# Decoder layer on one core: the feed-forward's W2 sums move to the retention's PSUM bank, W is split in another order, and TensorE transposes the identity in its waits

## What is computed

```python
x = layernorm(x + retention(x))        # 16 heads, decay mask, group norm per head, silu gate, wo
x = layernorm(x + mamba(ctx, z=x))     # conv 4, softplus step, 16 states, scan over 256 tokens
x = layernorm(x + moe_lora(x))         # W1, W3, W2 (F = 896), top 2 of 8 experts of rank 32

# retention
scores = einsum('bhnd,bhmd->bhnm', q, k) * dmask
ret = einsum('bhnm,bhmv->bhnv', scores, v)
norm = (ret - mean) * rsqrt(var + EPS) * gn_w + gn_b
out = silu(x @ wg + bg) * norm @ wo + bo
# mamba, per token
state = state * exp(d_t * A) + (d_t * u_t) * B_t;  y_t = sum(state * C_t)
y = (y + D * u) * silu(z)
# feed-forward, for each of the two experts e of a token, with its weight rw
x1 = x @ W1.T + lora1_e(x);  x3 = x @ W3.T + lora3_e(x);  x2 = silu(x1) * x3
out += (x2 @ W2.T + lora2_e(x2)) * rw
```

## Time and profile before

| | us |
|---|---|
| timed runs, median of 3 (lowest, highest) | 475.28 (475.27, 477.44) |
| the profiled execution, whole | 477.86 |
| the profiled execution, span from first to last instruction | 476.1 |
| mean granted TensorE clock in it | 0.934 |

### The profile page before, as it was taken

One profiled execution on the slowest core, in us unless ns is written; L12 is line 12 of the kernel. 1 busy time (PEld: TensorE's weight loads), 2 busy tenths in 40 slices (PEclk: granted clock), 3 DMA queues, 4 the chain that ended last, 5 costly groups with the idle time before them and its releaser, 6 DMA issues.

```text
span 476.1 us, 6961 instructions
## 1 busy us (share of the span) xinstructions
PE 410.4 (86%) x2488; PEld 336.6 (71%) x2488; DVE 340.3 (71%) x630; ACT 209.8 (44%) x497; POOL 231.6 (49%) x214
## 2 busy tenths in 40 slices
PE   3879674499899979997999979998999798799993
PEld 2645554367678968875779877876789687699992
DVE  3445975835889997768989996778889985632224
ACT  2699672547453332458534323476623322221010
POOL 5054766403936775116764954047566851041221
PEclk9989757759899999999999989999999989979999
DMA  6958040030013220030112220020121200000000
GB/s 227 140 223 326 2 154 22 0 92 23 1 46 88 76 69 23 1 92 23 45 66 70 66 61 19 17 86 12 67 89 44 67 1 1 0 23 1 1 1 23
DMA packets 14531, 28.46 MB, mean 60 GB/s; under 512 B 1816, under 2 KB 5152, under 8 KB 14240
## 3 DMA queue, kind: packets, MB, share of 16 engines
q1 hardware_dynamic: 13440, 23.26, 16.9%
q10 hardware_dynamic: 1056, 4.75, 2.7%
HBM read 26.56 MB, written 1.44 MB: 59 GB/s over the span
## 4 chain that ended last, share of the span: by engine, by line
PE 48%; DVE 26%; issue 13%; ACT 7%; POOL 3%; DMA 1%; SPq 1%; POOLq 0%; DVEq 0%; ACTq 0%
PE gen L880 14%; PE xf L880 14%; DVE ring L1427 10%; PE acc L880 8%; PE a2p L880 8%; PE ret L880 3%; DVE fth L1658 2%; DVE ring L1437 2%; ACT decay L597 2%; DVE ring L1486 1%; DVE cv L1369 1%; DMA wattn_sb<-in_wattn 1%; DVE work L1669 1%; POOL ring L497 1%; POOL wsplit L460 1%
## 5 line engine op out<-in xcount | busy, mean ns | idle before, releaser
L880 PE MATMUL xf<-am,wsplit 128*128 128x256 f32 x672 | 99.5, 300 | 0.0
L880 PEld LDWEIGHTS xf<-am,wsplit 128*128 128x128 f32 x672 | 89.2, 199 | 4.9 <-issue 4.3
L453 POOL TENSOR_TENSOR ring<-cv,brow 128x512 f32<-128x512 f32 x48 | 75.7, 1594 | 20.0 <-PE acc L880 19.7
L597 ACT ACTIVATE decay<-dt_w,nega 128x255 f32<-128x255 f32 x128 | 57.7, 500 | 58.1 <-DVE ring L1427 51.5
L1427 DVE TENSOR_TENSOR_SCAN ring<-decay,ring 128x512 f32<-128x512 f32 x48 | 76.5, 1593 | 0.0
L566 POOL TENSOR_TENSOR work<-work,ratioT 128x256 f32<-128x256 f32 x28 | 29.9, 1067 | 74.5 <-DVE work L1669 62.8
L880 PE MATMUL a2p<-work,wff_sb 128*128 128x256 f32 x224 | 60.4, 394 | 3.1 <-POOL work L566 3.1
L845 ACT ACTIVATE fth<-xf 128x256 f32<-128x256 f32 x56 | 21.1, 376 | 88.9 <-PE xf L880 88.9
L880 PE MATMUL acc<-ident,ring 128*128 128x128 f32 x256 | 41.3, 291 | 19.1 <-DVE ring L1437 10.7
L880 PEld LDWEIGHTS acc<-ident,ring 128*128 128x128 f32 x256 | 31.6, 148 | 31.7 <-DVE ring L1437 15.1
L880 PE MATMUL xf<-x2s,wsplit 128*128 128x256 f32 x336 | 50.7, 302 | 2.0 <-ACT ratioT L828 2.0
(11 more groups left out here) (201 smaller groups left out, 664.3 us busy)
## 6 DMA issues: line engine op xcount, KB each, us to landing
brow<-bc_dram SPq DMA_DIRECT2D x24, 256.0 KB, 3.6
crow<-bc_dram SPq DMA_DIRECT2D x24, 256.0 KB, 3.4
work<-in_wsp SPq DMA_DIRECT2D x2, 896.0 KB, 6.6
wff_sb<-in_wff SPq DMA_DIRECT2D x2, 896.0 KB, 8.3
work<-in_wsp ACTq DMA_DIRECT2D x2, 896.0 KB, 4.7
am<-bc_dram ACTq DMA_DIRECT2D x1, 1536.0 KB, 8.8
wattn_sb<-in_wattn SPq DMA_DIRECT2D x1, 1280.0 KB, 5.6
xT_sb<-in_xT SPq DMA_DIRECT2D x4, 256.0 KB, 3.8
```

The costliest lines, as they stand in the source:

```text
L453: pool.tensor_tensor(ring[:, i % RING], du[:, j].unsqueeze(1).broadcast_to([P, UN, S]), brow[:, c % 2], ALU.mult).then_inc(sem["drive_read ...
L597: act.activation(decay[:, i % 2, n, 1:], delta[:, j, 1:], ACT.Exp, scale=nega[:, j, s_:s_ + 1]).then_inc(sem["decay_ready"], 1)
L880: return pe.matmul(o, l, r, skip_group_check=True, **kw)
```

## The change

- `down` and `end_sum` sum W2's and B2's part in `ret`. `ret` is free once `norm_lin` has read it, in step 7 or so, so the sums for blocks 0 to 4 move into steps 9 to 12 (`DOWNS`), blocks 5 and 6 stay in the seam. The first `values` of a batch waits for the read of `ret` two batches back.
- The transposed routing waits for `crossed`'s read of `acc` (r2_ready), no longer for VectorE's end sum. In the last stage the spread ratios go to the bank `acc` (`xf_bank`), and `base(fb, 1)` stands ahead of them.
- The states' sums follow a table of their own, `SUMS`, one step later for the second of a pair. `times_c` of unit 15 moves from step 11 to 12.
- ScalarE's `start_y` moves from behind the first tanh to ahead of `am_high(fb, (2, 3))`; x2T is copied ahead of the convolution's tanh.
- Splitting in batch 0: B3 comes in four blocks into `keep`, `xsum`, `cv` and `u` and needs no `fetch`; the high parts of W1 and W3 are VectorE's, those of B3 and B1 ScalarE's; GpSimd makes 13 low parts, two ahead of its loop and the others in its steps, VectorE three of B1's behind `z_gate`. The copy of `spreadw` stands ahead of `bc_out`'s wait, so that W3 can be loaded sooner. The next batch's convolution input waits for 12 low parts.
- Batch 0's group norm, gated product, `attention_out`, `attended` and root stand one to four steps earlier.
- `keep_warm(o, n)`: TensorE transposes the identity n times into a free bank. Nobody reads it. 5 times in steps 8 to 13 of `first`, 10 and 12 times around the flip of x2 in batch 0's seam, 10 times behind the logits in the other seams.

```diff
-FF_PIECES = [("W1",), ("W3",), ("A1", "A3"), (), ("A2",), (), ("W2",), ("B2",)]
+FF_PIECES = [("W1",), ("W3",), ("B3",), ("A1", "A3"), ("A2",), ("W2",), ("B2",)]
+XF_BANK_LAST = [1, 0, 2, 0, 2, 2] + [(m + 1) % 2 for m, _ in MAIN]
+def xf_bank(fb, i):
+    return (XF_BANK_LAST if fb == B - 1 else XF_BANK)[i]
-HIGH_ACT = {3: (0, 0), 4: (0, 1), 5: (0, 2), 6: (0, 3), 12: (2, 0), 13: (2, 2)}
-LOW_POOL = {4: (0, 0), 5: (0, 1), 6: (0, 2), 7: (0, 3), 13: (2, 0), 14: (2, 2)}
+HIGH_DVE = {1: (1, 0), 2: (1, 1), 3: (1, 2), 4: (1, 3)}
+HIGH_ACT = {5: (3, 0), 6: (3, 1), 7: (3, 2), 8: (3, 3), 9: (2, 0), 10: (2, 1), 11: (2, 2), 12: (2, 3)}
+LOW_POOL = {0: (0, 2), 1: (0, 3), 2: (1, 0), 3: (1, 1), 4: (1, 2), 5: (1, 3),
+            8: (3, 0), 9: (3, 1), 10: (3, 2), 11: (3, 3), 12: (2, 0)}
 SCANS = [[0], [1], [2], [3, 4], [5], [6], [7], [8, 9], [10], [11, 12], [13, 14], [15], [], []]
+SUMS = [[], [0], [1], [2], [3], [4, 5], [6], [7], [8], [9, 10], [11], [12], [13, 14], [15]]
+DOWNS = {9: (0,), 10: (1, 2), 11: (3,), 12: (4,)}
...
# SyncE
+                        if i == 3:
+                            sp.wait_ge(sem["c_first0"], 16)
+                            sp.wait_ge(sem["duT_filled"], 1)
+                            sp.wait_ge(sem["bT_filled"], 1)
+                            need(sp, "y_init", 0, 2)
+                            for c in range(PER_W):
+                                sp.dma_start(b3_raw[c][:, 0:BLOCK], wsp[3][:, c * BLOCK:(c + 1) * BLOCK]
+                                             ).then_inc(sem["w_rawb"], 16)
...
# GpSimd, first
+                split_low(0, 0)
+                split_low(0, 1)
                 masked(b, 2)
                 masked(b, 3)
                 for i in range(UNITS):
                     first_times_c(b, i)
-                    if i == 7:
+                    if i == 6:
                         root(b, gvar, grs, "gn_step", 9, "gn_pow")
-                    if i == 10:
                         gated(b)
-                    if i == 13:
+                    if i == 11:
                         root(b, ve, rs, "r1_ready", 7, "r1_pow")
...
                 root(b, ve, rs, "r2_ready", 9, "r2_pow")
-                for c in range(PER_W):
-                    split_low(3, c)
...
# ScalarE, later and seam
                     decays(b, 0)
+                if b is not None:
+                    need(act, "dt_step", b, 3)
+                    start_y(b)
                 am_high(fb, (2, 3))
...
+                need(act, "xf_filled", b, X_X2 + 1)
+                act.activation(x2T[:], xf[XF_BANK[X_X2]][:], ACT.Copy).then_inc(sem["x2T_ready"], 1)
                 if nb is not None:
                     conv_tanh(nb)
...
# TensorE
-                    mm(acc[:, t], xsums[m][:, t * P:(t + 1) * P], W2[:, m], start=(m == 0 and t == 0), stop=False)
+                    mm(ret[:, t], xsums[m][:, t * P:(t + 1) * P], W2[:, m], start=(m == 0 and t == 0), stop=False)
+            def keep_warm(o, n):
+                for _ in range(n):
+                    pe.transpose(o[:, 0:P], ident[:], ident[:])
...
# TensorE, first
-                    if i == 11:
+                    if i == 9:
                         attention_out(b)
-                    if i == 15:
+                    if i == 8:
+                        need(pe, "gn_step", b, 9)
+                    if 8 <= i <= 13:
+                        keep_warm(gen[G_VAR % 2], 5)
+                    if i == 14:
                         token_z(b)
+                context(nb)
                 add_states(b, UNITS - 1)
-                seam(b, None, nb)
+                need(pe, "x_in", nb, 16)
+                project(nb, "Q", wq)
+                seam(b, None, None)
+                low_rank(nb)
...
# TensorE, seam
                 if fb is not None:
-                    need(pe, "r2_ready", b, 2)
-                    for m in range(4):
-                        down(fb, m)
+                    down(fb, FM - 2)
+                else:
+                    pe.wait_ge(sem["dub_ready"], NT * DS)
+                    keep_warm(a2p[0][:, 0], 10)
                 flip_x2(b)
                 if fb is not None:
-                    for m in range(4, FM):
-                        down(fb, m)
+                    down(fb, FM - 1)
+                else:
+                    keep_warm(a2p[0][:, 0], 12)
                 logits(b)
+                if fb is not None:
+                    need(pe, "a2_ready", fb, 1)
+                    keep_warm(a2p[0][:, 0], 10)
...
# TensorE, stage
-                            for i in SCANS[n - 1]:
+                            for i in SUMS[n]:
                                 add_states(b, i)
...
                         if n == 9:
                             attention_out(b)
+                            need(pe, "ro_lin", b, 2)
+                        for m in DOWNS.get(n, ()):
+                            down(fb, m)
...
# VectorE, first
+                for c in range(PER_W):
+                    split_high(0, c)
...
                 z_gate(b)
+                for c in range(1, PER_W):
+                    split_low(2, c)
```

115 lines of the change are left out of this document (59 added, 56 removed).

## The result

| | before | changed |
|---|---|---|
| timed beside each other, median of 4 (lowest, highest), us | 476.36 (475.27, 477.96) | 459.16 (456.85, 461.82) |
| ratio, 95% interval | | 0.9638 (0.9575 to 0.9701) |
| profiled execution, whole, us | 477.86 | 458.83 |
| its span, us | 476.1 | 457.1 |
| mean granted clock in it | 0.934 | 0.976 |

The change takes 3.6% off, 17.2 us where 29.0 were forecast; 459.16 lies 1.2 us over the upper end of the range of all cases (458) and 9.2 over the forecast's own (450). In the profiled executions the span fell by 19.0 us.

The account below looks back on a forecast made before the run. Five stretches had different limits: loads, ScalarE and TensorE; GpSimd's scans; the seam; TensorE and VectorE; TensorE. Savings of 5.9 + 3.5 + 2.2 + 5.3 + 6.0 + 2.4 + 3.7 = 29.0 from 475.28 gave 446.3 us, range 441.5 to 450.

Parts of the forecast that it names:

- Splitting W: Batch 0: with low parts spread over GpSimd's steps, y is read at 77.2 and not 83.12; 5.9 us saved.
- Convolution: First seam: with no low part left beside it, the convolution goes from 5.95 to 2.46 us; 3.5 us saved.
- Clock in seam and stage 1: Identities hold TensorE's clock in the first seam (2.2 us) and stage 1 (5.3 us).
- They stand where TensorE waits: Batch 0 and its seam: the identities lie in TensorE's waits for GpSimd and for x2, 0.11 us each at full clock.
- `start_y`: Stage heads: one place earlier on ScalarE, yT is ready as `hidden(0)` ends; 2.0 us in each of three stages.
- W2 sums and states' sums: Five W2 sums moved into steps 9 to 12 bring `step_size` 1.2 us sooner in seams 1 and 2.
- Cost nothing: Loops: the states' sums, one step later for the second of a pair, were said to cost no time.
- 0.9 to spare: Steps 9 to 12: TensorE has 19.6 us for 18.7 of work with five W2 sums in, so they stay hidden.
- Last seam and last feed-forward: End of kernel: logits and routing flip come sooner, `base(1)` skips the ratios' wait, `hidden(2)` ends at 422.0; 3.7 us saved.
- The clock rival: Batch 0 to stage 1: identities don't hold the clock, about 10.7 us lost, 457 us; chance 0.25.
- The loops take the head start back: Stages: VectorE and GpSimd hold each other up; `start_y` and seams give 2.4 and not 8.4, 452 us; chance 0.17.
- The slower one: Steps 9 to 13: TensorE's queue ends them at half clock, adding 15 us a stage, 491 us; chance 0.03.

Follow-up runs that it names:

- f1: Changed kernel with, in the first seam, 26 identities ahead of the flip of x2, five behind it, nine behind the logits; 456.47 us, ratio 0.9548.
- k1: Changed kernel with 26 identities added ahead of the flip of x2 in first and last seams, last seam's ten behind the logits left out; 450.80 us.
- f4: Changed kernel with ScalarE's `start_y` put back behind the first tanh; 467.31 us, ratio 0.9803.
- f3: Changed kernel with the states' sums at their old places, pairs one step earlier; 468.69 us, ratio 0.9834.
- k4: Changed kernel with 26 identities ahead of the flip of x2 in the last seam alone, its ten behind the logits left out; 457.80 us, ratio 0.963.
- f2: Changed kernel with three W2 sums back in the last seam and its ten identities left out; 455.96 us, ratio 0.9567.
- e3: Changed kernel with W2 sums 2, 3 and 4 back in the last seam, ahead of the flip of x2; 455.61 us, ratio 0.9542.

## Why the prediction missed

Forecast and trace are 10.0 us apart in the span (447.1 and 457.1). The other 2.9 us of the 12.9 come nearly all from the base: the saving was worked out against an execution of 477.86 us and taken from a median of 475.28, which lies below all six later medians of before (475.4 to 478.0; the first of them still has those three runs in it). With each term of the forecast taken off before's cut, the 10.0 are 1.2 for the read of y, 1.5 for the first seam, 2.1 for stage 1, 0.5 for stage 2, and 4.7 from stage 3's `step_size` to the end.

- *Splitting W (5.9; measured 4.7, and 2.5 to 5.0 in the variants).* The mechanism was right, and the term was mis-sized by 1.2. The four copies ahead of the first scan, put at nothing, waited 1.38 us for W1 and took 3.18, not 1.5; the first scan began at 28.90 and not 26.53, and the group statistics were there at 50.7 and not 49.8. That these 0.9 us come from the copies is likely but not shown. GpSimd's gated product ended at 58.6 and not 57.9, and its last three products took 4.17 and not 3.72, the last of them beside VectorE's low parts. In 8 of the 18 profiles of changed kernels TensorE had lost its clock in 76 to 80 us, which made the stretch from the gated product to the read of y 1.2 to 1.7 us longer.
- *Convolution (3.5).* Right: 2.46 us.
- *Clock in seam and stage 1 (7.5).* This step failed. "They stand where TensorE waits" was taken for "they fill the wait": ten identities are 1.25 us, and 2.10 us stayed open. Counted against the wait, they would have shown it. f1 and k1 with the gap filled have 9.8 and 9.65 us for the seam (9.3 forecast) and 99.3 for the stage (98.7 forecast): the gain was there and the count was too small. The twelve ahead of the logits were costed at nothing and took 2.77 us in front of them.
- *`start_y` (3 x 2.0).* Right: f4 gives 2.1 a stage.
- *W2 sums and states' sums (2 x 1.2).* The seam came out at 12.88 for 13.98, a gain of 1.1. "Cost nothing" for the later sums was wrong in both directions. Between scan 4 and the last scan stage 2 takes 40.5 us for 39.5 before; 0.7 of it is their cost, since f3 takes 39.8. And they are what keeps the loop from losing by the W2 sums: undone they cost 2.4 us in stage 2 (f3) and 9.5 in the total, so the "0.9 to spare" was theirs, since my sum of TensorE's queue left out its waits for VectorE's products with C. Behind the last scan the changed kernel takes 7.4 us for 7.9. Net that is the 0.5 us by which stage 2 missed.
- *Last seam and last feed-forward (3.7; measured a loss of 0.6).* The largest miss, 4.3 us, and a failed step: what leaves a queue leaves a gap. I counted the sums out of the seam and asked what came sooner, and for seams 1 and 2 that was right, since there the projection fills the wait but for 0.76 us. The last seam has no projection; 3.35 us stood open, and 380 to 391 us ran at half clock. The moved sums gain nothing there even when the clock holds: 75.9 us with them in the loop (k4), 76.0 with three in the seam (f2). e3 gives 76.9 us, a gain of 3.7: the sum held wherever the clock did. The ten behind the logits I did count, at full clock.
- *Rivals.* The clock rival's 457 is near the number, but for another reason: its mechanism, that transposes don't hold the clock, is refuted by f1 and k1. "The loops take the head start back" had 6 us; it was 0.4 to 0.5 a stage, 1.4 in all. The slower one did not occur; its price was also mis-added, since 19 us at 1.9 times their length are 17 us more and not 15.

k1, the change with these two gaps closed, has a span of 449.1 us, 2.0 over the forecast's 447.1: 1.1 for the read of y, 0.3 for the first seam, 0.5 for each of stages 1 and 2, less 0.5 for the rest, where the ten identities (0.9) are left out.
